# Relative attention scores: the realigning transfers take rows 34 partitions apart instead of 32

## The reference, cut to what matters

```python
x = x + 0.5 * ffn(layernorm(x))             # x: [2, 2048, 256]
# attention, 16 heads of 16:
AC = einsum('bhid,bhjd->bhij', q + u_bias, k)
BD = einsum('bhid,hjd->bhij', q + v_bias, rp)   # rp: 4095 relative positions
BD = _rel_shift(BD)                         # BD[i, j] = q_i . rp[j - i + L - 1], with its zero column and wrap
attn = softmax((AC + BD) / 4)
x = x + attn @ v                            # [b, h, i, j] @ [b, h, j, d]
x = x + 0.5 * ffn(layernorm(x))
```

## Time and profile before

| | |
|---|---|
| median of 3 executions | 3639.61 us (3603.37 to 3652.35) |
| the profiled execution | 3635.0 us, span 3633.2 us |
| mean granted TensorE clock | 0.918 of full |
| busy TensorE (matmul) / VectorE / ScalarE / GpSimd | 3101.9 / 2491.0 / 2592.2 / 2399.6 us |
| transfers `score<-to_move` | 4096, 128 KB each, median 6.6 us from issue to landing |
| data moved by DMA | 688.16 MB, of which 537.92 MB on GpSimd's queue |

### The profile page before, as it was taken

The page is one execution under the profiler, slowest core; times in us unless marked ns, Lnnn a source line. Parts: engine busy times, 40 slices in busy tenths (PEclk is TensorE's granted clock), DMA queues, the critical chain, the costliest instruction groups (busy, mean ns, idle before and its releaser), DMA issues. The chain is left out here.

```text
span 3633.2 us, 116111 instructions
## 1 busy us (share of the span) xinstructions
PE 3101.9 (85%) x40768; PEld 2111.4 (58%) x40768; DVE 2491.0 (69%) x4784; ACT 2592.2 (71%) x4110; POOL 2399.6 (66%) x4232
## 2 busy tenths in 40 slices
PE   4665399999989999989999998998998999999945
PEld 1444066666656666656666666666665666666634
DVE  1555077777777777768777777777776777877845
ACT  2333378878877787778788788787887788888822
POOL 3224567777777777777777777777776777877700
PEclk8777599999999999999999999999999999999977
DMA  8233899999989999998999998999998999999831
GB/s 247 87 98 107 184 190 212 207 202 206 213 194 204 203 201 201 199 204 193 202 209 207 202 204 205 201 201 199 208 216 182 206 208 206 212 199 209 204 103 40
DMA packets 473336, 688.16 MB, mean 189 GB/s; under 512 B 296752, under 2 KB 394928, under 8 KB 404144
## 3 DMA queue, kind: packets, MB, share of 16 engines
q0 software_dynamic: 327680, 537.92, 69.9%
q1 hardware_dynamic: 145072, 142.63, 16.0%
HBM read 90.06 MB, written 52.43 MB: 39 GB/s over the span
## 5 line engine op out<-in xcount | busy, mean ns | idle before, releaser
L646 POOL DMA_DIRECT2D score<-to_move x4096 | 2268.0, 562 | 802.7 <-PE pt_bank L819 687.4
L876 ACT COPY to_move<-pos_bank 128x512 f32<-128x512 f32 x2048 | 1088.5, 611 | 579.7 <-PE pos_bank L752 390.3
L886 ACT ACTIVATE score<-score,low 128x1024 f32<-128x1024 f32 x1024 | 1213.4, 1186 | 37.4 <-issue 25.6
L819 PE MATMUL pt_bank<-ident_sb,score 128*128 128x128 f32 x8192 | 1141.0, 281 | 49.6 <-issue 44.7
L819 PEld LDWEIGHTS pt_bank<-ident_sb,score 128*128 128x128 f32 x8192 | 975.3, 144 | 339.9 <-DVE prob_t L946 90.1
L937 DVE CUSTOM_DVE_ANT_0 score<-ac_bank,score 128x1024 f32<-128x1024 f32 x512 | 627.2, 1225 | 701.2 <-PE ac_bank L805 667.4
L946 DVE COPY prob_t<-pt_bank 128x512 f32<-128x512 f32 x1536 | 1009.2, 685 | 16.1 <-PE pt_bank L819 14.2
L937 DVE CUSTOM_DVE_ANT_0 score<-ac_bank,score,low 128x1024 f32<-128x1024 f32 x512 | 656.6, 1282 | 141.0 <-PE ac_bank L805 139.4
L752 PE MATMUL pos_bank<-pos,qv 96*32 96x512 bf16 (+15 forms) x12160 | 647.5, 322 | 122.5 <-DMA qv<-qv_parts 57.4
L833 PE MATMUL acc_bank<-prob_t,vs 128*32 128x128 f32 x16384 | 687.5, 284 | 33.2 <-issue 33.0
L805 PE MATMUL ac_bank<-ks,qu 96*128 96x512 bf16 x2048 | 639.5, 395 | 25.2 <-issue 19.3
(11 more groups left out here) (94 smaller groups left out, 974.3 us busy)
## 6 DMA issues: line engine op xcount, KB each, us to landing
score<-to_move POOLq DMA_DIRECT2D x4096, 128.0 KB, 6.6
pos<-pos_parts SPq DMA_DIRECT2D x192, 128.0 KB, 9.9
pos_parts<-part SPq DMA_DIRECT2D x32, 384.0 KB, 4.2
ks<-k_parts SPq DMA_DIRECT2D x192, 64.0 KB, 5.1
qu<-qu_parts SPq DMA_DIRECT2D x768, 16.0 KB, 8.0
qv<-qv_parts SPq DMA_DIRECT2D x576, 16.5 KB, 7.0
v_heads<-v_sb SPq DMA_DIRECT2D x8, 1024.0 KB, 7.3
vs<-v_heads SPq DMA_DIRECT2D x32, 256.0 KB, 10.5
```

The lines of the kernel that those rows point to most:

```text
L646: pool.dma_start(score[s::QUAD, dst:dst + FT, :], to_move[s::QUAD, src:src + FT, QUAD - 1 - s:QUAD - 1 - s + L])\
L819: last = pe.matmul(PT[c % 2][:, t * P:(t + 1) * P], lhsT=score[:, slot(k), c * BANK + t * P:c * BANK + (t + 1) * P], rhs=ident_sb[:, :], i ...
L876: act.copy(to_move[:, at + f, c * BANK:(c + 1) * BANK], ring(m)[:, :]).then_inc(pos_out, 1)
L886: act.activation(cols, cols, ACT.Exp, bias=low[:, slot(k), NH - 1:NH], scale=-1.0)\
```

## The change

The quads' own shift is changed by 2 columns for each quad further down (LEAN = 2), so that rows with the same residual shift now lie 34 partitions apart (STRIDE). A `line` names the first of them; lines from -6 to 31 exist, 38 in all. 26 lines hold four rows, four hold three, four hold two and four hold one row. So a group takes 38 transfers, which carry the same 128 rows of 4 tiles. They are issued in an order written out by hand. The residual shift goes up to 37, so the last item of a group is 38 columns wide for each tile instead of 32, and the position table is padded by 16 zero columns at each side, by four small memsets for which TensorE waits once.

```diff
             QUAD = 32
-            MWIN = L + QUAD
-            CLUSTER = 4
-            MOVE_ORDER = [CLUSTER * c + i for i in range(CLUSTER) for c in range(QUAD // CLUSTER)]
+            LEAN = 2
+            STRIDE = QUAD + LEAN
+            SHIFTS = QUAD + 3 * LEAN
+            MWIN = L + SHIFTS
+            PAD = 16
+
+            def rows_of(line):
+                held = [q for q in range(4) if 0 <= line + LEAN * q < QUAD]
+                first = line + STRIDE * held[0]
+                return slice(first, first + STRIDE * (len(held) - 1) + 1, STRIDE)
+            MOVE_ORDER = [2, 10, 18, -6, 0, 8, 16, 24, 3, 11, 19, -5, 1, 9, 17, 25,
+                          6, 14, 22, 30, 4, 12, 20, 28, -4, 7, 15, 23, 31, 5, 13, 21, 29, -3,
+                          26, -2, 27, -1]
...
-            pos = [s2(f"pos{u}", [STACK, NPOS], BF16) for u in range(2)]
+            pos = [s2(f"pos{u}", [STACK, PAD + NPOS + PAD], BF16) for u in range(2)]
...
+                for u in range(2):
+                    pool.memset(pos[u][:, 0:PAD], 0.0).then_inc(padded, 1)
+                    pool.memset(pos[u][:, PAD + NPOS:], 0.0).then_inc(padded, 1)
...
-                    for s in MOVE_ORDER:
-                        pool.dma_start(score[s::QUAD, dst:dst + FT, :],
-                                       to_move[s::QUAD, src:src + FT, QUAD - 1 - s:QUAD - 1 - s + L])\
+                    for line in MOVE_ORDER:
+                        rows, shift = rows_of(line), QUAD - 1 - line
+                        pool.dma_start(score[rows, dst:dst + FT, :], to_move[rows, src:src + FT, shift:shift + L])\
                             .then_inc(moved[j % DST], 16)
...
-                        split = min(max((i + 1) * P - moves - first, 0), width)
-                        at = (NI - 1 - i) * P + moves + first
+                        at = (NI - 1 - i) * P + moves + first - LEAN * (row // QUAD)
+                        split = min(max(L - at, 0), width)
...
+                pe.wait_ge(padded, 4)
...
-                                 ring(m)[:, 0:FT * QUAD].rearrange("p (f w) -> p f w", w=QUAD)).then_inc(pos_out, 1)
+                                 ring(m)[:, 0:FT * SHIFTS].rearrange("p (f w) -> p f w", w=SHIFTS)).then_inc(pos_out, 1)
```

More of the change, by code:

```diff
@@ L525, in build_program @@
             QUAD = 32
-            MWIN = L + QUAD
-            CLUSTER = 4
-            MOVE_ORDER = [CLUSTER * c + i for i in range(CLUSTER) for c in range(QUAD // CLUSTER)]
+            LEAN = 2
[10 more added lines that the diff above has]
+                          26, -2, 27, -1]
+            assert sorted(MOVE_ORDER) == list(range(-3 * LEAN, QUAD))
             FT = 4
@@ L566, in build_program @@
             moved = [sem(f"moved{i}") for i in range(DST)]
+            padded = sem("padded")
             pos_full, pos_out = sem("pos_full"), sem("pos_out")
@@ L573, in build_program @@
             NLOAD = 16 * len(Q_PARTS)
+            MOVES = 16 * len(MOVE_ORDER)
             def tile_steps(eng, body, past):
@@ L658, in _, with load_stacked @@
             def _(sp):
-                def load_stacked(dst, src, order, hd, lo, n, loaded):
+                def load_stacked(dst, src, order, hd, lo, n, loaded, at=0):
                     for i, part in enumerate(order):
-                        sp.dma_start(dst[i * DH:(i + 1) * DH, 0:n],
+                        sp.dma_start(dst[i * DH:(i + 1) * DH, at:at + n],
                                      src[part, bass.ds(hd * DH, DH), lo:lo + n]).then_inc(loaded, 16)
@@ L677, in load_pos @@
                 def load_pos(step, h):
-                    load_stacked(pos[h % 2], pos_parts, K_PARTS, head(step, h), 0, NPOS, pos_loaded[h % 2])
+                    load_stacked(pos[h % 2], pos_parts, K_PARTS, head(step, h), 0, NPOS, pos_loaded[h % 2], PAD)
                 def load_vs(step, h):
@@ L753, in quads @@
                                                  lhsT=qv[k // FT % 2][:, q0:q0 + QUAD],
-                                                 rhs=pos[u][:, at + lo:at + hi], start=True, stop=True)
+                                                 rhs=pos[u][:, PAD + at + lo:PAD + at + hi], start=True, stop=True)
                     return last
@@ L776, in positions @@
                         for f in range(FT):
-                            last = quads(ring(m), f * QUAD, step, j * FT + f, L, QUAD)
+                            last = quads(ring(m), f * SHIFTS, step, j * FT + f, L, SHIFTS)
                     last.then_inc(pos_full, 1)
@@ L871, in take @@
                     if m == 0 and group_there(step, j - SRC):
-                        act.wait_ge(moved[(j - SRC) % DST], use_of_dst(step, j - SRC) * (16 * QUAD) + 16 * QUAD)
+                        act.wait_ge(moved[(j - SRC) % DST], use_of_dst(step, j - SRC) * MOVES + MOVES)
                     act.wait_ge(pos_full, group(step, j) * ITEMS + (m + 1))
@@ L931, in add @@
                     if h == 0 and k % FT == 0:
-                        dve.wait_ge(moved[k // FT % DST], use_of_dst(step, k // FT) * (16 * QUAD) + 16 * QUAD)
+                        dve.wait_ge(moved[k // FT % DST], use_of_dst(step, k // FT) * MOVES + MOVES)
                     if h:
```

## The result

The changed kernel takes 4614.24 us in the median (4576.69 to 4649.01), against 3640.68 us before: a ratio of **1.264**, 95% interval 1.2585 to 1.27. The ratio is that of the fast executions; one of the four of the changed kernel, at 4649.01 us, was a slow one and is left out of it. The forecast was 3580 us. The profiled execution has a span of 4574.9 us.

What follows compares the result with a forecast made beforehand. A two-group loop of copies, issue and transfer tail was taken to bound the kernel. From 3635.0 us, periods of 23.05 instead of 23.81 gave -97, smaller terms +28, +10, +12, +3, -10: 3581, stated as 3580 us, 8-in-10 range 3465 to 3690.

Steps and rivals of the forecast that it cites:

- the part on the rows 34 apart and the new order: GpSimd's moves: same bytes, DMA time for a group between 13.7 and 19.6 us, taken as about 17.
- my own loop: ScalarE copies, GpSimd start, issue, tail span two groups: 37.4 us plus tail before, 46.3 us after, 23.1 a period.
- why is the tail long: Landing of a group's moves: mean tail 10.2 us, from a DMA backlog of 4.7 us and about 5.5 us latency.
- The issue price: GpSimd: a fixed 0.554 us for each transfer, short ones taken nearly whole, so 38 issues take 21.05 us.
- The rival of cheap short transfers: GpSimd: issue priced at least partly by rows, 19.4 us a group half way; 3480 to 3530 us, chance 0.20.
- The floor of 23.05 us: GpSimd's own pace for a group after the change: 21.05 us of issue plus 2.00 us.
- The 2.00 us between groups: GpSimd: taken as the time of the two waits between groups, added to the issue time.
- 17.4 us: ScalarE: mean time from first copy to last copy of a group, one term of the two-group period.
- The issue's own cost on the path: Two-group period: issue grows from 17.7 to 21.05 us while the tail falls from 10.2 to about 5.5 us.
- no-effect rival: GpSimd's moves: DMA work stays 22.4 us, tail about 7, period 23.9 us; 3640 us, no change, chance 0.13.
- The slower rival: Two-group period: longer issue added, tail stays 8.5 us or more, period 24.6 us; +105 us, 3740 us, chance 0.12.
- The clock: TensorE: granted clock should rise a little if its stalls become short and even.

Runs made afterwards that it cites:

- 2 + 2: Kernel before, own order and spacing, but six of the 32 transfers cut into two of two rows each, 38 issues: 3789.25 us.
- 3 + 1: Kernel before, own order and spacing, but six of the 32 transfers cut into three rows and one, 38 issues: 4040.46 us.
- the sorted order: Changed kernel with its spacing and 38 transfers, reordered so each DMA engine keeps meeting the same places, rotated in a cycle of four groups: 3901.7 us.
- G: Bursts without computation: transfers of the kernel before, in its order, every fifth cut in two of two rows: 67.9 us for three groups.
- H: Bursts without computation: transfers of the kernel before, in its order, every fifth cut in three rows and one: 70.8 and 76.1 us for three groups.

## Why the prediction was wrong, step by step

**The step that failed** is in the part on the rows 34 apart and the new order: "The bound above is the present 19.6 us for a group" of DMA time. It was no bound. I treated DMA time as bytes times a price that the spacing could only lower, and took the order as harmless, though it stood in the diff and I said nothing on what it removes. Measured are 27.0 us, above both ends: a DMA engine moved 201.61 MB / (0.867 x 1500 x 16 us) = 9.7 GB/s while busy, where it was 13.3 by the same rows before. Everything else follows by my own loop: 19.6 became 27.0, the backlog grew instead of vanishing, and the period went to 31.15 us. 127 periods longer by 7.34 us are 932 us; the span grew by 942.

**The reading of "why is the tail long"** was right (a backlog of DMA work), but I didn't ask why 19.6 us and not 27 or 46. The runs show that the order of before is a good one of many: 46.4 us of DMA time in plain sequence, 22.2 in the order of the change, 19.7 in its own. The reason that I argue for is the turn of the DMA engines. Two pairs of runs went the way that this predicts: 2 + 2 against 3 + 1 (3789 and 4040, where 4100 or more was expected), and the sorted order against the given one (3902 and 4614). Which engine carried which packet no trace here shows, so the assignment itself is argued and not shown.

A rival stands untested: **rows in flight together**, whichever engine carries them. The order 0, 1, 2 puts neighbouring rows in flight together, and the first 16 transfers of the change's order, but for two single rows, keep to lines 0 to 3, 8 to 11, 16 to 19 and 24 to 25, while the old order and my sorted one go through the whole range of lines in every eight or so. That sorts 19.7, 22.2 and 46.4 us, and the sorted order too, without any turn. Only 2 + 2 against 3 + 1 and G against H keep the places and move the turn, and there the packets of the single rows explain an estimated 1.0 of 2.5 us. So it is shown that the order and the shapes set the DMA time, and not what share of it is the turn.

**The issue price** was right: "a fixed part", 0.57 us for a lone transfer of four rows and 0.53 to 0.55 for fewer, 20.97 us for 38 against 21.05 forecast. The rival of cheap short transfers falls.

**The floor of 23.05 us** was wrong, without effect on the outcome. The 2.00 us between groups is no fixed price of the two waits: the first two groups of the kernel before stand in one run of 64 issues in 35.59 us; in the 2 + 2 kernel groups follow after 0.28 and 0.60 us, and in the changed kernel 1.46 us of idle time stands inside a group, after 14 issues, and 0.38 between groups. What sets this gap stays open.

**The loop** held. One of the two copies behind its 17.4 us (1778.44) had waited for TensorE and not for transfers, so before the change it didn't bind in every group; with 108 waits it does in most. That misreading changed little.

**The issue's own cost on the path.** I let six more issues be paid by a shorter tail. In the 2 + 2 kernel the landing did fall (5.4 us in the median, from 6.4), yet the time rose by 140 us, beside a new wait of TensorE for the `qu` loads, 180 us. I had named SyncE's loads as something that crowds the moves, and not asked who crowds SyncE.

**The spacing** brought in a transfer alone what it promised, 4.0 against 5.1 us, and nothing in a burst (62.0 against 59.5 us for three groups, and no less DMA time behind the issue) or in the kernel (+2%). My own no-effect rival, "the spacing does nothing for the DMA time", holds for the spacing by itself.

**The slower rival** had the right sign and the right point, a tail above 6.9 us, and it looked at the short transfers. Its mechanism, that they "fall unevenly on the DMA engines", isn't what the trace shows: in 1400 to 1900 the 16 engines are busy 1.00 of the time, and it is the packets that last longer. I priced it at +105 us, with a tail of 8.5, and argued it away: "the backlog is there now and must shrink when the same work is fed in more slowly". The work wasn't the same. Its size came from no row but from a wish to stay near the present tail.

**The clock** went the other way than forecast, 0.85 instead of 0.95 in 1400 to 1900, where TensorE is busy for 383 of 500 us instead of 461.

## What to carry to other kernels

When many small SBUF-to-SBUF transfers keep the DMA engines busy, their DMA time isn't bytes times a price: the same 32 transfers cost 19.7, 22.2 or 46.4 us by their order alone. When DMA time rises, look also at who else uses the engines: two of these kernels got new waits for loads that nobody had touched. Before such an order is touched, or a transfer put in that takes another number of rows than its neighbours, measure a burst of them alone, more than once; a small kernel shows it without any computation. And a bound from the present value is a bound only for what the change can't make worse.

## What the runs showed of the hardware that I had not expected

- A transfer of two rows (28 and 62) takes 5.1 us alone and one of four rows (2, 36, 70, 104) takes 4.0 us.
- The order alone moves the DMA time of the same transfers by a factor of 2.4 (19.7 and 46.4 us).
- The burst in the order 0 to 31 took 117 us the first time; the second time it was issued from 881.20 on, and the store that waits for all of it began at 950.47, so it took at most 69 us. A burst in a bad order has more than one course; what decides between them stays open.
- GpSimd's issue price hardly depends on the rows of a transfer (0.53 us for one row, 0.57 us for four).
- A lone transfer of one row goes out as four packets at once, each 1.17 to 1.53 us long, where a packet of four rows that share no port takes 0.31 to 0.55 us.
